# Routing of tokens to experts: from two stages of its own into the turns of the attention

## What is computed

```python
h = concat([image_tokens(x), text_encoder(x_txt)], axis=1)      # 8 x 561 x 192; 49 image and 512 text tokens
h = h + attention(layernorm(h), ...)                            # 12 heads of 64, own token masked out
x = layernorm(h).reshape(-1, 192)                               # 4488 tokens
probs = softmax(x @ gate_w)                                     # 8 experts
top_w, top_i = top_k(probs, 2)                                  # both weights go into combine
y = gelu(x @ w_up[e] + b_up[e]) @ w_down[e] + b_down[e]         # 192 -> 768 -> 192, for the chosen experts
h = h + sum over the chosen experts of y * weight
```

## Time and profile before

| | us |
|---|---|
| median of the runs (3) | 4368.94 |
| the profiled execution, its own time | 4374.97 |
| its span | 4373.2 |
| TensorE busy | 3810.5 (87%) |
| VectorE busy | 2232.9 (51%) |
| ScalarE busy | 2119.3 (48%) |
| GpSimd busy | 1101.8 (25%) |

### The profile page before, as it was taken

The page is one execution under the profiler, slowest core; times in us unless marked ns, Lnnn a source line. Parts: engine busy times, 40 slices in busy tenths (PEclk is TensorE's granted clock), DMA queues, the critical chain, the costliest instruction groups (busy, mean ns, idle before and its releaser), DMA issues. The chain is left out here.

```text
span 4373.2 us, 64449 instructions
## 1 busy us (share of the span) xinstructions
PE 3810.5 (87%) x21850; PEld 2532.1 (58%) x21850; DVE 2232.9 (51%) x3419; ACT 2119.3 (48%) x3230; POOL 1101.8 (25%) x1004
## 2 busy tenths in 40 slices
PE   4899999999999999999856999999999996408998
PEld 2455555555555555555534677666766774307887
DVE  6566666666666666666524444444444442213443
ACT  0554554554555545545414766755756663003332
POOL 5132332322332322323210000000000001063444
PEclk7899999999999999999977999999999998558999
DMA  7333233242343342333114111111111112335664
GB/s 174 93 101 105 87 106 102 87 117 87 90 119 93 94 117 79 101 108 92 48 48 116 31 34 27 31 35 23 35 31 24 37 28 96 103 112 161 148 145 107
DMA packets 265492, 368.62 MB, mean 84 GB/s; under 512 B 49616, under 2 KB 166400, under 8 KB 261824
## 3 DMA queue, kind: packets, MB, share of 16 engines
q1 hardware_dynamic: 232752, 285.52, 23.1%
q0 software_dynamic: 22960, 57.40, 5.8%
q10 hardware_dynamic: 9600, 23.26, 1.6%
HBM read 235.77 MB, written 116.32 MB: 81 GB/s over the span
## 5 line engine op out<-in xcount | busy, mean ns | idle before, releaser
L641 DVE TENSOR_REDUCE mx<-ring 128x2 f32<-128x1024 f32 x768 | 920.0, 1223 | 505.8 <-PE ring L404 502.8
L533 ACT ACTIVATE probs<-ring 128x1024 f32<-128x1024 f32 x768 | 767.2, 1024 | 418.0 <-PE ring L417 417.0
L1430 DVE TENSOR_REDUCE a_nmx<-a_ring 128x1 f32<-128x561 f32 (+1 forms) x480 | 341.6, 737 | 309.1 <-PE a_ring L1271 158.9
L1320 ACT ACTIVATE a_ring<-a_ring,a_nmx 128x561 f32<-128x561 f32 (+1 forms) x480 | 333.8, 695 | 197.8 <-DVE a_nmx L1430 194.8
L404 PE MATMUL ring<-k_stack,q_stack 48*128 48x512 f32 x1536 | 360.0, 481 | 63.5 <-ACT probs L533 23.1
L417 PE MATMUL ring<-q_stack,k_stack 64*128 64x512 f32 x1536 | 363.5, 490 | 51.9 <-DVE mx L641 39.2
L431 PE MATMUL acc<-probs,vals 128*32 128x512 f32 x3072 | 400.6, 642 | 1.3 <-ACT probs L533 1.3
L1201 POOL TENSOR_SCALAR_AFFINE_SELECT a_probs<-a_probs 128x256 f32<-128x256 f32 (+1 forms) x240 | 91.9, 383 | 1227.4 <-ACT a_probs L1352 1227.4
L1352 ACT ACTIVATE a_probs<-a_ring 128x561 f32<-128x561 f32 (+1 forms) x480 | 287.4, 637 | 169.2 <-PE a_ring L1268 166.4
L1268 PE MATMUL a_ring<-a_k_hh,a_q_hl 128*128 128x256 f32 (+1 forms) x960 | 311.1, 339 | 22.6 <-DVE a_q_hl L1410 11.0
L417 PEld LDWEIGHTS ring<-q_stack,k_stack 64*128 64x128 f32 x1536 | 142.6, 189 | 285.9 <-DVE mx L641 102.0
(11 more groups left out here) (220 smaller groups left out, 6801.8 us busy)
## 6 DMA issues: line engine op xcount, KB each, us to landing
q_stack<-qk_scratch SPq DMA_DIRECT2D x576, 64.0 KB, 2.3
k_stack<-qk_scratch SPq DMA_DIRECT2D x576, 64.0 KB, 2.4
qk_scratch<-qk_hi SPq DMA_DIRECT2D x32, 768.0 KB, 3.6
qk_scratch<-qk_lo SPq DMA_DIRECT2D x32, 768.0 KB, 5.1
a_q_hm<-a_q_hl SPq DMA_DIRECT2D x48, 280.5 KB
a_k_hh<-a_k_hh SPq DMA_DIRECT2D x48, 280.5 KB
tokens<-h_out SPq DMA_DIRECT2D x33, 384.0 KB, 2.5
h_in<-tokens SPq DMA_DIRECT2D x32, 384.0 KB, 4.3
```

The source lines that it names most:

```text
L533: nc.scalar.activation(probs[n % 2][:, pair:pair + 2, x // 2, :], buf[:, :, :], ACT.Exp, scale=DK ** -0.5).then_inc(act, 1)
L641: nc.vector.tensor_reduce(mx[s][:, i, :].rearrange("p (r t) -> p r t", r=2)[:, :, t], buf[:, :, :], AX, ALU.max).then_inc(dve, 1)
L1320: nc.scalar.activation(buf, buf, ACT.Exp, bias=nmx[0:r, i, h:h + 1], accum_out=sums[0:r, i, h:h + 1]).then_inc(act, 1)
L1430: nc.vector.tensor_reduce(nmx[0:r, i, h:h + 1], flat(buf)[0:r, 0:N], AX, ALU.max, negate=True).then_inc(dve, 1)
```

## The change

1. Route and place are gone. Their work is a new stream r of 80 steps in the attention's order. For the batch that has just been projected, each step is one link: moments, 1/sqrt on GpSimd, normalised rows into `r_xw`; then ten pairs of a product (GpSimd, 128 x 768: one tile with four experts' gate vectors) and a sum (VectorE, 768 to 4); then softmax (exponential on ScalarE), rank, choice; a job "count" on TensorE; running counts, slots; ten indirect scatters. `A_ORDER` without its r letters is the old one with one w fewer: the projections of tiles 3 and 4 are one step.
2. Blocks are given out as they fill: each expert holds a current block across batches, and takes new ones by number when it overflows, so slots are known batch by batch. A row carries all eight weights, and the blocks phase picks its own by a product and a sum (two instructions where one copy was). There are 25 blocks as before.
3. The last batch is routed in `A_CLOSE`, after the last projection, with nothing beside it.
4. The copies into the experts' table go to SyncE's queue in the encoder's last turn; the blank rows of `slots_in` and the pad of `fused` too, after the encoder's R_FINAL. They are waited for at the end of the encoder.
5. The start of the attention: batch 0 is loaded first, the arrays that the first steps need have a semaphore of their own, GpSimd clears `a_q_hm`, VectorE writes `a_k_l` once, with ones.

```diff
@@ encoder, SyncE
+                        if s == 1 and R is R_FINAL:
+                            build_table()
...
+            sp.wait_ge(blank, 1)
+            sp.dma_start(lane, dram["lane"]).then_inc(lane_in, 16)
             steps(R_FINAL, 0)
+            sp.wait_ge(blank, 2)
+            for n in range(NBLOCKS):
+                sp.dma_start(slots_in[n * BLOCK:(n + 1) * BLOCK, :].rearrange("(p i) d -> p i d", i=4), empty).then_inc(filled, 16)
+            sp.dma_start(fused[B * N:B * N + BLOCK, :].rearrange("(p i) d -> p i d", i=4), empty[:, :, 0:D]).then_inc(filled, 16)
             store(R_CLOSE, 0, 0, 6, 0)
             store(R_CLOSE, 0, 1, 7, len(CLOSE))
+            sp.wait_ge(made, 16 * 7)
+            sp.wait_ge(filled, 16 * (NBLOCKS + 1))
@@ encoder, VectorE
+            nc.vector.memset(empty, 0.0).then_inc(blank, 1)
+            steps(R_FINAL, 0)
+            v.wait_ge(blank, 1)
+            v.wait_ge(lane_in, 16)
+            for i in range(4):
+                ins = nc.vector.tensor_scalar(empty[:, i, D:D + 1], lane, 4.0, float(B * N + i), ALU.mult, ALU.add)
+            ins.then_inc(blank, 1)
@@ the order of the attention
-A_ORDER = "qqvweevewemsqvmvsmmsmssqevmwswmesweeeemmsmpsmsms...
+A_ORDER = "qqvweevewemsqvmvsmmsmssqevmwsmeswreereemmsmpsmsmsmsrspermmsrspreemrserqmprmsrpesrpmrsmsrqeerlsrpperqprxemresrmsprqpremsreerelermsmrqprmsermprsmsrsmrpsqrmersmprseeremremsrspremsmepseremrmpsrsqrmemrssmrsqrseprperqxqreprmmsrsmrspereemrsmrspereerpepremrmsmrsprsmsrmmsrmsreesrmsrmmsrpmrssermprseeremrepprsemrsmrseerserpeprperxpprprr"
+ROUTE = ([("r", x) for x in ("stats", "rsqrt", "norm")] + [("r", x, j) for j in range(10) for x in ("mult", "add")]
+         + [("r", x) for x in ("top", "less", "exp", "total", "inv", "share", "gt", "eq", "tie", "over", "rank", "mark", "is_k", "sel")]
+         + [("count",)] + [("r", "weight")] + [("r", "run", i) for i, _ in TILES]
+         + [("r", x) for x in ("pos", "new1", "new2", "cum", "ends", "past", "first", "taken", "offset", "delta", "high", "high_by",
+                               "in_cur", "in_new", "pick", "slot_f", "slot", "rest", "cur1", "cur2", "cur3", "cur4", "own1", "own2",
+                               "own3", "own4")]
+         + [("scatter", i, k) for i, _ in TILES for k in range(2)])
-A_CLOSE = [("wo", i) for i, _ in TILES]
+A_CLOSE = [("wo", i) for i in range(4)] + ROUTE
@@ attention, SyncE at ("take", 0)
                             sp.wait_ge(stored, per_batch(R, it, 32, BASE))
+                            await_step(sp, R, it, "route", ("r", "norm"), now)
@@ attention, GpSimd
+                    elif step[:2] == ("r", "mult"):
+                        j = step[2]
+                        await_step(g, R, it, "route", ("r", "add", j - 1) if j else ("r", "norm"), now)
+                        row = xw[:, j // 2:j // 2 + 1, 0:D].to_broadcast([P, 4, D])
+                        nc.gpsimd.tensor_tensor(prod[:, :, :], row, gate[:, 4 * (j % 2):4 * (j % 2) + 4, :], ALU.mult).then_inc(route, 1)
+                    elif step[0] == "scatter":
...
+                        g.indirect_dma_start(slots_in, bass.IndirectOffsetOnAxis(ap=slot[0:r, k, i:i + 1], axis=0),
+                                             xw[0:r, i, :], None).then_inc(scattered, 16)
@@ attention, VectorE
+                elif what == "norm":
+                    v.wait_ge(rst2, per_batch(R, it, 2, 0))
+                    if R is not R_SECOND:
+                        v.wait_ge(scattered, per_batch(R, it, 160, -160))
...
+                elif what == "add":
+                    j = step[2]
+                    after("mult", j)
+                    ins = add_up(logits[:, j // 2, 4 * (j % 2):4 * (j % 2) + 4], prod[:, :, :], AX, ALU.add)
@@ attention, TensorE
+                    elif kind == "count":
+                        await_step(pe, R, it, "route", ("r", "sel"), now)
+                        for k, t in enumerate((before, ones)):
+                            last = nc.tensor.matmul(buf[:, k, 0:5 * E], t[:, :], sel[:, :, :].rearrange("p i e -> p (i e)"),
+                                                    start=True, stop=True)
@@ blocks, VectorE
-                        nc.vector.tensor_copy(part[:, n, :], x[n % XS][:, :, D + 1])
+                        nc.vector.tensor_tensor(parts[:, n, :, :], x[n % XS][:, :, D + 1:D + 1 + EXPERTS],
+                                                mine[:, n:n + 1, :].to_broadcast([P, 4, EXPERTS]), ALU.mult)
...
+                        nc.vector.tensor_reduce(part[:, n, :], parts[:, n, :, :], AX, ALU.add).then_inc(shared, 1)
@@ build: route_phase and place_phase are gone
```

More of the change, by code:

```diff
@@ L982, in batch_steps @@
     streams = {
-        "w": [("wo", i) for i, _ in TILES],
+        "w": [("wo", i) for i in range(4)],
         "v": [("v", i) for i, _ in TILES],
@@ L1042, in rows_of, with attention_phase @@
     return (v[:, 0:4 * P, :].rearrange("b (i p) d -> b p i d", p=P)[b], v[:, 4 * P:N, :][b])
[L1045 removed]
+def attention_phase(nc, dram, tokens, fused, slots_in, which, mine):
     start = {n: BASE for n in Attention.names}
@@ L1086, in attention_phase @@
         half = sb("a_half", [P, 5])
+        E = EXPERTS
+        gate = sb("r_gate", [P, E, D])
+        lane = sb("r_lane", [P, 1])
+        invalid = sb("r_invalid", [P, 1])
+        before = sb("r_before", [P, P])
+        ones = sb("r_ones", [P, P])
+        upto = sb("r_upto", [P, E, E])
+        numbers = sb("r_numbers", [P, NBLOCKS])
+        xw = sb("r_xw", [P, 5, XW])
+        stats2 = sb("r_stats", [P, 5, 6])
+        mv2 = sb("r_mv", [P, 5, 2])
+        rstd2 = sb("r_rstd", [P, 5])
@@ new lines, in attention_phase @@
+        var_eps2 = sb("r_var_eps", [P, 5])
+        prod = sb("r_prod", [P, 4, D])
+        in_prod = prod[:, :, :].rearrange("p e d -> p (e d)")
+        gate_raw = vals[:, 0:2, :, :].rearrange("p i h d -> p (i h d)")
+        logits = sb("r_logits", [P, 5, E])
+        top = sb("r_top", [P, 5])
+        pr = sb("r_pr", [P, 5, E])
+        total = sb("r_total", [P, 5])
+        over, same = (in_prod[:, 5 * E * E * k:5 * E * E * (k + 1)].rearrange("p (i e f) -> p i e f", e=E, f=E) for k in range(2))
@@ new lines, in attention_phase @@
+        past = in_prod[:, 0:NBLOCKS * E].rearrange("p (n e) -> p n e", e=E)
+        cum = in_prod[:, 10 * E * E:11 * E * E].rearrange("p (e f) -> p e f", f=E)
+        rank = sb("r_rank", [P, 5, E])
+        is_k = sb("r_is_k", [P, 2, 5, E])
+        sel = sb("r_sel", [P, 5, E])
+        count = sb("r_count", [P, 2, 5, E])
+        part = sb("r_part", [P, 2, 5, E])
+        run = sb("r_run", [P, 6, E])
+        place = sb("r_place", [P, 5, E])
+        high = sb("r_high", [P, 5, E])
+        one, new, ends, first, offset, delta, current, begin = (sb(f"r_{n}", [P, E]) for n in (
+            "one", "new", "ends", "first", "offset", "delta", "current", "begin"))
@@ L1212, in _ @@
                 steps(R_LOOP, it)
-            steps(R_FINAL, 0)
+            for R in (R_FINAL, R_CLOSE):
+                steps(R, 0)
+            g.wait_ge(scattered, 160 * B)
         @block.tensor
@@ L1326, in steps @@
                         nc.scalar.activation(logs[:, :, :], sums[:, :, GH * g:GH * g + GH], ACT.Ln).then_inc(act, 1)
+                        continue
+                    if step == ("r", "exp"):
+                        await_step(sc, R, it, "route", ("r", "less"), now)
+                        nc.scalar.activation(pr[:, :, :], logits[:, :, :], ACT.Exp).then_inc(act, 1)
                         continue
@@ L1388, in steps, with name_blocks @@
+            def name_blocks():
+                v.wait_ge(route, R_CLOSE.end()["route"])
+                ts(which[:, :], owner[:, :], float(P), lane[:, 0:1], ALU.mult, ALU.add)
+                tt(mine[:, :, :], owner[:, :].rearrange("p (n a) -> p n a", a=1).to_broadcast([P, NBLOCKS, E]),
+                   numbers[:, 0:E].rearrange("p (a e) -> p a e", a=1).to_broadcast([P, NBLOCKS, E]), ALU.is_equal).then_inc(route, 1)
             def steps(R, it):
@@ L1390, in steps @@
                     kind = step[0]
-                    if kind == "ln":
+                    if kind == "r" and step[1] not in ("rsqrt", "exp", "mult"):
+                        route_step(R, it, step, now)
+                    elif kind == "ln":
                         (moments, normalise)[step[1]](R, it)
```

595 lines of the change are left out of this document (274 added, 321 removed).

## The result

The changed kernel took 4206.25 us (median; 4202.79 to 4209.09), the kernel before 4368.56 in the same comparison: ratio 0.9629, 95% interval 0.9614 to 0.9645, faster. Forecast were 4180 us and a range of 4150 to 4230. They add up to 172.1 us, the medians of the runs to 162.3: the profiled execution before was 6.4 us slower than its median, the one after 3.5 us faster than its own, and no view says in which stretch these 9.9 us lie.

A forecast was written before the change was run, and what follows sets the result against it. Latency (transfers, chains, issue) was taken to bound the stretches between TensorE's busy phases. Terms -190 - 25 + 2 + 24.5 = -188.5 us took the median 4368.94 to 4180 us, range 4150 to 4230.

The forecast's parts named there:

- Route and place go, the last batch's routing comes: Between attention and blocks: 257.7 us removed, 67.8 us of last-batch routing added behind the last projection, saving 190 us.
- The start: At the attention's start: fewer, earlier clears and a free ScalarE bring the first products 25 us earlier.
- Table and blank rows: In the encoder: the copies and fills hide in idle transfer time, costing only 2 us.
- Rival D: In the encoder: copies at half speed end 26 us behind it, 4206 us in total; chance 0.06.
- Blocks: In the blocks phase: one more small VectorE instruction a block, hidden under TensorE, 0 us.
- Seven turns: In the attention's seven turns with routing: TensorE delayed 3.5 us a turn, 24.5 us in all.
- Sums late 2, VectorE waiting for a product 0.5: Per turn: ten sums each late by some 0.2 us cost 2 us, VectorE's occasional waits for products 0.5 us.
- Scatters and masks 0.5: At a turn's end: scatters bunched, six ahead of the last mask, make GpSimd about 0.5 us late.
- rival A: In the turns: sums delay reductions by their length, scatters take 1.69 us each; 10 us a turn, 4226 us; chance 0.12.
- rival B: In the turns: routing is free but for TensorE's 0.5 us a turn, 4159 us; chance 0.10.
- E: In the turns: VectorE stands at every sum and the ring runs dry, 56 us a turn, 4555 us; chance 0.03.
- Rival C: In the turns: a two-tile SBUF subtraction on VectorE stands for a whole 1.80 us product, 4193 us; chance 0.07.

The follow-up runs named there:

- exchange of two places: Version with two product buffers, scatters behind the masks and later clear, its seventh sum moved behind VectorE's share of the shift: 4154.86 us, ratio 0.9520.
- the run with both short: Changed kernel with GpSimd's products and VectorE's sums in the turns cut to 8 of each 192 columns: 4183.08 us, ratio 0.9591.

## Why the prediction was right, and where it was off

The forecast was 4180 us and the median came to 4206.25, 26 us over it and inside the range. Against the forecast the turns took 20 us more and the blocks 2.5; the encoder's end came 6.4 us earlier than forecast, and another 9.9 us are the distance of the two profiled executions from their medians. That the encoder's end offset part of the miss was luck.

*Route and place go, the last batch's routing comes: -190.* Right, each term within 1 us; the links came 0.7 us short and the landing 1.0 long, which cancel.

*The start: -25.* Right, -24.5, and for the reasons named: earlier clears and a free ScalarE. The run with the copy put back shows that without the second the first brings nothing; it doesn't show that the second alone would have brought all.

*Table and blank rows: +2.* Hidden, as said, with the store 9 us earlier than estimated. Rival D is out.

*Blocks: 0.* +2.5 us; two later profiles, of the changed kernel again and of the exchange of two places, have +2.0 and +1.2. The cause wasn't followed.

*Seven turns: +24.5.* This is the step that failed: 44.5 us. The mechanism was the one named and the parts were priced too low:
- Counts 0.5: measured 0.5.
- Sums late 2, VectorE waiting for a product 0.5: together 4.0 by the run with both short. I took a sum to be late by 0.2 us and the waits as rare. But with one buffer GpSimd can't begin a product before the sum in front of it, so VectorE stood 4.3 us a turn; and the cost of a sum hangs on what stands behind it: nothing is lost up to the landmark behind the first three, and TensorE waited 1.0 us for the shift's share behind the seventh.
- Scatters and masks 0.5: measured 1.26, a scatter and a fraction in front of the last mask.

The rest, 0.6 of the 6.4, I did not trace. The bound (every sum late by its whole length, 10 us a turn) was not reached, so rival A is out as priced, though the truth lies between it and the forecast; rival B (turns free) is out, E nowhere near. A also took the scatters at 1.69 us each; the 70 in the turns took 0.98 us on average. E's 4555 is a slip of 5 us: seven times 56.3 in place of the 24.5 gives 4550.

*Rival C* asked whether products and VectorE get in each other's way. VectorE's groups in the turns, before and after (mean ns of one behind the busy time):

```profile
L1430 DVE TENSOR_REDUCE a_nmx<-a_ring 128x1 f32<-128x561 f32 x326 | 235.6, 739 | 256.0 <-PE a_ring L1268 128.2 <-PE a_ring L1271 126.3
L1396 DVE TENSOR_TENSOR a_shift<-a_nmx,a_logs 128x20 f32<-128x20 f32 x21 | 3.8, 179 | 33.1 <-ACT a_logs L1326 33.1
```

```profile
L1738 DVE TENSOR_REDUCE a_nmx<-a_ring 128x1 f32<-128x561 f32 x320 | 232.9, 738 | 145.6 <-PE a_ring L1398 80.9 <-PE a_ring L1401 62.7
L1704 DVE TENSOR_TENSOR a_shift<-a_nmx,a_logs 128x20 f32<-128x20 f32 x20 | 4.7, 232 | 28.9 <-ACT a_logs L1465 28.9
```

The maxima are as long as before with ten products beside them. The subtraction of two SBUF tiles grew from 179 to 232 ns: 0.16 us a turn, since there are three of them and not one as I wrote, and not 1.8. Rival C is out by its size.

## What to carry to other kernels

Work moved under a busy engine costs by its position in the queue that it joins: ask for each added instruction what stands behind it and who waits for that, and look at the producer too, since a consumer that waits for it holds up all that stands behind, and for longer than its own length. Where two engines pass work to and fro, a second buffer frees the consumer where the order lets the producer run ahead. And ScalarE, while it issued the long copies, was a busy engine, though the table of busy times doesn't count it: look for such an issue ahead of a first instruction that is late.

## What the runs showed of the hardware

A GpSimd clear of 128x1040 numbers (0.97 us, no input) that began 0.08 us ahead of five normalisations on VectorE made them 2.49 us long, and so within 0.01 us in all seven profiles in which this clear alone fell beside them; with the clear elsewhere they took 1.58 or 1.59 in three, and 1.53 before the change. One of the five took 1344 ns where the median one took 367: the difference is the clear's length. In the run with both short, where one more clear and then the gate's copy on GpSimd (2.73 us) fell beside them, the five took 5.67 us, and one of them 2865 ns. The Trainium skill (SBUF — State Buffer, "Who interferes with whom") says that a tile-by-scalar VectorE instruction in a two-port mode and GpSimd hold a port pair in turn for a whole instruction, and that a reduction never contends. The first agrees with these times, though no view shows the mode; the second with the maxima above, 739 and 738 ns. I had applied the rule only to two-input instructions beside products.

GpSimd's clear of 128x6744 took 5.72 us, about as long as VectorE's 5.68, 0.85 ns a number, while its product of two inputs took 1.80 us for 768 numbers, 2.3 ns a number.
